# Edge loop of a graph layer: three banks for the edge products, one softmax step per item, key rows from DRAM, sums two places later

## The reference, cut to what matters

```python
q, k, v = x @ Wq + bq, x @ Wk + bk, x @ Wv + bv       # per node
e = edge_attr @ We                                      # per edge
kj = k[src] + e
alpha = einsum('ehc,ehc->eh', q[dst], kj) / sqrt(C)
amax = segment_max(alpha, dst)
ea = exp(alpha - amax[dst])
denom = segment_sum(ea, dst)
msg = (v[src] + e) * (ea / (denom[dst] + 1e-16))[:, :, None]
out = segment_sum(msg, dst) + (x @ Ws + bs)
```

## Time and profile before

| | us |
|---|---|
| Median of three runs | 2544.61 |
| Profiled execution, its own time | 2543.3 |
| Its span | 2541.5 |
| TensorE busy | 2375.7 |
| VectorE busy | 2029.1 |
| GpSimd busy | 1809.0 |
| ScalarE busy | 1573.9 |
| Edge loop, first to last projection | 224.8 to 1925 |

### The profile page before, as it was taken

How to read it: one execution, slowest core, us unless ns; L and a number is a source line. 1 busy time by engine, 2 the same in 40 slices (tenths; PEclk the granted TensorE clock), 3 DMA queues, 4 the chain that set the end, 5 groups by cost and what they waited for, 6 DMA issues and landing times. The chain is left out here.

```text
span 2541.5 us, 61885 instructions
## 1 busy us (share of the span) xinstructions
PE 2375.7 (93%) x13314; PEld 1998.8 (79%) x13315; DVE 2029.1 (80%) x5248; ACT 1573.9 (62%) x4349; POOL 1809.0 (71%) x2136
## 2 busy tenths in 40 slices
PE   6998999999999999999999999999996658999998
PEld 3445888888888888888888888888884647999998
DVE  6865999999999999999999999999997873222222
ACT  1223677776777677777777777776775115666665
POOL 4213788888888888888888888888886204666666
PEclk9999999999999999999999999999998558999999
DMA  7326777777777777777778777777772672433443
GB/s 233 129 106 197 234 229 224 228 228 224 223 228 228 219 229 228 223 228 226 228 226 230 228 223 228 226 228 215 230 225 82 203 215 57 71 63 64 69 67 54
DMA packets 337727, 476.35 MB, mean 187 GB/s; under 512 B 61382, under 2 KB 268556, under 8 KB 337116
## 3 DMA queue, kind: packets, MB, share of 16 engines
q0 software_dynamic: 92576, 259.72, 38.4%
q1 hardware_dynamic: 238556, 213.23, 27.7%
q10 hardware_dynamic: 6288, 0.05, 0.1%
HBM read 425.40 MB, written 50.57 MB: 187 GB/s over the span
## 5 line engine op out<-in xcount | busy, mean ns | idle before, releaser
L809 POOL DMA_INDIRECT kv_ring<-vk_table,tab_c x880 | 860.0, 977 | 274.9 <-issue 176.5
L967 PE MATMUL ps_e<-we_sb,aT 128*128 128x256 f32 x3520 | 917.8, 384 | 23.8 <-DVE ve_ke L1055 19.9
L967 PEld LDWEIGHTS ps_e<-we_sb,aT 128*128 128x128 f32 x3520 | 602.0, 191 | 95.6 <-issue 46.3
L1050 DVE TENSOR_TENSOR ve_ke<-kv_ring,ps_e 128x512 f32<-128x512 f32 x880 | 599.7, 681 | 34.1 <-PE ps_e L971 22.7
L819 POOL TENSOR_TENSOR ve_ke<-ve_ke 128x256 f32<-128x256 f32 x880 | 551.2, 630 | 16.5 <-ACT factor L936 3.0
L1020 PE MATMUL ps_u<-ve_ke,sel 128*128 128x264 f32 x1760 | 545.3, 392 | 17.0 <-POOL ve_ke L819 6.1
L971 PE MATMUL ps_e<-q_slots,selT 128*128 x1760 | 517.5, 375 | 0.0
L896 ACT COPY aT<-ps_t 128x256 f32<-128x256 f32 x880 | 325.4, 370 | 294.6 <-PE ps_t L951 255.3
L1126 DVE SCALAR_TENSOR_TENSOR node_slots<-node_slots,same_tile,ps_u 128x264 f32 x880 | 422.6, 480 | 25.5 <-PE ps_u L1020 21.4
L971 PEld LDWEIGHTS ps_e<-q_slots,selT 128*128 128x128 f32 x1760 | 335.3, 191 | 45.1
L1038 DVE TENSOR_REDUCE alpha<-ve_ke 128x8 f32<-128x256 f32 x880 | 362.4, 412 | 1.9
(11 more groups left out here) (251 smaller groups left out, 2630.3 us busy)
## 6 DMA issues: line engine op xcount, KB each, us to landing
a_ring<-in_edge_attr SPq DMA_DIRECT2D x880, 128.0 KB
loc_c<-loc_table SPq DMA_DIRECT2D x220, 128.0 KB, 4.4
kv_ring<-vk_table,tab_c POOLq DMA_INDIRECT x880
vk_table<-kv_out SPq DMA_DIRECT2D x49, 256.0 KB, 2.0
skip_table<-skip_out SPq DMA_DIRECT2D x49, 128.0 KB, 1.7
skip<-skip_table SPq DMA_DIRECT2D x7, 896.0 KB, 9.3
xn_table<-node_slots SPq DMA_DIRECT2D x7, 896.0 KB, 5.1
w_sb<-in_L_ffn_W SPq DMA_DIRECT2D x2, 2048.0 KB, 10.3
```

The lines of the kernel that those rows point to most:

```text
L809: g.indirect_dma_start(out=kv_ring[:, i % N_KV, :], out_offset=None, in_=vk_table, in_offset=bass.IndirectOffsetOnAxis(ap=tab_c[:, c % N_T ...
L967: t.matmul(ps_e[i % 2][:, 0:D], aT[i % 2][:, k * P:(k + 1) * P], we_sb[:, k, :], start=(k == 0), stop=(k == KD - 1))
L1050: v.tensor_tensor(ve_ke[:, to:ke + 1:ke - to, 0:D], kv.rearrange("p (t d) -> p t d", t=2), e[:, None, :].to_broadcast([P, 2, D]), ALU.add) ...
```

## The change

- `N_E = 3`: the edge products go to three banks in turn, `ps_e[(c * CH + i) % 3]`, and a projection waits for VectorE's reads of the item three back.
- All softmax products share one bank `ps_s`: the scores, then the minima; the turned result takes the place of the scores.
- The key rows are no longer turned by TensorE. The first section writes two tables of 8 values per item to DRAM (`first_table`, `last_table`), and SyncE loads them, spread over the partitions, once per chunk into `key_c`. The previous chunk's last key is part of that row, so `key_prev` goes.
- `minima` has two transposes and one product of 8 columns where it had three transposes.
- Places: TensorE from keys 0, scores 3, minima 6, turn_scores 10 to scores 4, minima 7, turn_scores 12. ScalarE's `exp` from 11 to 12. VectorE from scan 3, scan_back 4, own 6, least 7, shift 8 to scan 3, scan_back 4, own_first 6, own_last 7, least_first 8, least_last 9, shift 10.
- Lags: select from 11 to 13, sum and add from 13 to 15; weigh stays at 15.
- The addition is `source + ps_u`, where a second slot number per item names the source: the item's own node slot, or, at the first item of a node tile, a slot of zeros. The numbers are loaded as pairs, for two items at a time, within the score of an item.
- Later sections place some buffers over others; their instructions stay.

```diff
             LAG = dict(weigh=FIRST_WEIGH + N_KV,
-                       select=FIRST_WEIGH,
-                       sum=FIRST_WEIGH + 2,
-                       add=FIRST_WEIGH + 2)
+                       select=FIRST_WEIGH + 2,
+                       sum=FIRST_WEIGH + 4,
+                       add=FIRST_WEIGH + 4)
...
-                over_chunks(act, emit, what="select", parts={3: "apart", 4: "offs", 11: "exp"})
+                over_chunks(act, emit, what="select", parts={3: "apart", 4: "offs", 12: "exp"})
...
-                    pe.wait_ge(s["kq_ready"], at("kq_ready", c * CH + (i - 2)))
+                    pe.wait_ge(s["kq_ready"], at("kq_ready", c * CH + (i - N_E)))
...
-                            t.transpose(ps_r[:, KW - P:KW], min_l[par][:, 0:1].to_broadcast([P, P]), ident[:, :])
                             t.transpose(ps_r[:, 0:P], scan_b[:, 0:1].to_broadcast([P, P]), ident[:, :])
-                            t.transpose(ps_r[:, P:2 * P], scan_f[:, P - 1:P].to_broadcast([P, P]), ident[:, :])
+                            t.matmul(ps_r[:, P:P + H], min_l[par][:, 0:1].to_broadcast([P, P]), ident[:, P - H:P], start=True, stop=True)
+                            t.transpose(ps_r[:, P + H:KW], scan_f[:, P - 1:P].to_broadcast([P, P]), ident[:, :])
...
-                over_chunks(pe, emit, what="sum", parts={0: "keys", 3: "scores", 6: "minima", 10: "turn_scores"})
+                over_chunks(pe, emit, what="sum", parts={4: "scores", 7: "minima", 12: "turn_scores"})
...
+            def load_keys(sp, c):
+                keys = key_c[c % 2]
+                sp.dma_start(keys[:, 0:P], first_table[c * CH:(c + 1) * CH, :].rearrange("(o i) h -> o (i h)", o=1).to_broadcast([P, P])
+                             ).then_inc(key_loaded[c % 2], 16)
+                sp.dma_start(keys[:, P:KW], last_table[c * CH:(c + 1) * CH + 1, :].rearrange("(o i) h -> o (i h)", o=1).to_broadcast([P, P + H])
+                             ).then_inc(key_loaded[c % 2], 16)
...
+                then(v.scalar_tensor_tensor(out=from_rep[:, :], in0=node_tile_rep[:, :], scalar=float(NT + 2), in1=same_tile[:, :],
+                                            op0=ALU.subtract, op1=ALU.mult))
+                for h in range(2):
+                    row, some = slice(64 + 32 * h, 65 + 32 * h), slice(h * IT // 2, (h + 1) * IT // 2)
+                    v.tensor_copy(item_slots[h][:, :, 0], node_tile_rep[row, some])
+                    then(v.tensor_scalar(item_slots[h][:, :, 1], from_rep[row, some], float(NT + 2), None, ALU.add))
...
+                def slots_of(c, i):
+                    h, m = divmod(c * CH + i, IT // 2)
+                    both = nc.values_load_multi_w_load_instructions(
+                        item_slots[h][:, m:m + AT_ONCE, :].rearrange("p i k -> p (i k)"), engines=[mybir.EngineType.DVE],
+                        min_val=0, max_val=NT + 2, skip_runtime_bounds_check_because="a count of at most NT steps, or NT + 2")[1]
+                    return list(zip(both[0::2], both[1::2]))
...
-                    v.scalar_tensor_tensor(out=to, in0=sofar, scalar=same_tile[:, m:m + 1], in1=ps_u[i % 2][:, 0:UW], op0=ALU.mult, op1=ALU.add
-                                           ).then_inc(s["acc_added"], 1)
+                    v.tensor_tensor(to, sofar, ps_u[i % 2][:, 0:UW], ALU.add).then_inc(s["acc_added"], 1)
...
-                over_chunks(dve, emit, what="add", parts={3: "scan", 4: "scan_back", 6: "own", 7: "least", 8: "shift"})
+                over_chunks(dve, emit, what="add", parts={3: "scan", 4: "scan_back", 6: "own_first", 7: "own_last",
+                                                         8: "least_first", 9: "least_last", 10: "shift"})
```

More of the change, by code:

```diff
@@ L22 @@
 N_KV = 4
+N_E = 3
 N_A = 4
@@ L99, in gnn_ffn @@
         item_row = item_rows[32:33, :]
+        item_slots = [item_rows[64 + 32 * h:65 + 32 * h, :].rearrange("p (i k) -> p i k", k=2) for h in range(2)]
         chunk_tile = sb("chunk_tile", [P, NCH])
@@ L131, in gnn_ffn @@
         run_c = [sb(f"run_c{i}", [P, P], F32, c_soft) for i in range(2)]
+        KW = 2 * P + H
+        key_c = [sb(f"key_c{i}", [P, KW], F32, c_soft) for i in range(2)]
         resets = [sb(f"resets{i}", [P, P + 1], F32, c_soft) for i in range(2)]
@@ L136, in gnn_ffn @@
         reset_loaded = [sem(f"reset_loaded{i}", c_soft) for i in range(2)]
+        key_loaded = [sem(f"key_loaded{i}", c_soft) for i in range(2)]
         loc_loaded = [sem(f"loc_loaded{i}", c_soft) for i in range(NLOC)]
@@ L176, in gnn_ffn @@
             t_rep = sb1("t_rep", [P, IT])
+            from_rep = t_rep
             t_item = sb1("t_item", [P, IB])
@@ L313, in _ @@
                     if j == LOCS_OUT:
+                        with nc.allow_non_contiguous_dma(reason="eight head keys of an item"):
+                            keys_to_tables()
                         sp.wait_ge(tables_ready, LOCS)
@@ L1121, in add @@
-                def add(c, i, n, before):
+                AT_ONCE = 2
+                assert CH % AT_ONCE == 0 and IT // 2 % AT_ONCE == 0
+                def slots_of(c, i):
[4 more added lines that the diff above has]
+                    return list(zip(both[0::2], both[1::2]))
@@ L1129, in emit, with load_next @@
                 def emit(c, par, steps):
+                    adds = [(c - b, k) for kind, k, b in steps if kind == "add"]
+                    places = len([1 for kind, k, b in steps if kind == "score"])
+                    def load_next(place):
+                        if adds and place + len(adds) >= places:
+                            cc, k = adds.pop(0)
+                            if k % AT_ONCE == 0:
+                                ahead[:] = slots_of(cc, k)
                     for kind, i, back in steps:
@@ L1590, in gnn_ffn @@
             y_full = [sb7(f"y_full{i}", [P, D]) for i in range(2)]
-            y = [sb7(f"y{i}", [P, D]) for i in range(4)]
+            y = [values[:, i, :] for i in range(4)]
             ps_t = [c7.enter_context(nc.psum_tensor(f"ps_t7{i}", [P, 512], F32)) for i in range(2)]
```

140 lines of the change are left out of this document (73 added, 67 removed).

## The result

| | median us | range | runs |
|---|---|---|---|
| before | 2545.75 | 2544.28 to 2549.65 | 4 |
| after | 2585.91 | 2583.47 to 2587.03 | 4 |

The changed kernel is slower: ratio 1.0154, 95% interval 1.0136 to 1.0172. I had said 2529 (2500 to 2556), with 0.15 for slower. The profiled span is 2581.6 us, 40.1 longer than before.

What follows compares the result with a forecast made beforehand. TensorE and VectorE were taken as nearly full, with waits deciding. Per chunk 1.72 us go and 1.35 come, net -0.37, times 54 is -20.0; prologue and tail +3.6, together -16: 2529 us, range 2500 to 2556.

Steps and rivals of the forecast that it cites:

- The copy behind the exponentials: TensorE's projection 13 waits for ScalarE's copy 13, queued behind the exponentials: 1.25 us taken per chunk.
- X + 1.90: Forecast start of projection 13; X is the start of TensorE's sum after turn_scores, copy end X + 1.84 plus 0.06 us.
- Register loads: VectorE's eight loads of 4 slot numbers per chunk hide behind the wide addition: 0 us taken, bounds 0 to 2.8.
- The sums at lag 15 ... no sum for the weighing: TensorE's sum gets four places of slack behind GpSimd's weighing instead of two; the 0.38 us wait at place 3 goes.
- the second rival: VectorE stays as late; sums wait for the addition two items back, 0.3 us a chunk, time 2545; chance 0.14.
- The plain addition: VectorE's add takes 0.41 us instead of 0.480, saving 1.1 us a chunk.
- the 0.2 that I had taken off: On VectorE, one softmax step per item removes the wait of 0.2 us between the two own steps, an estimate.
- what was gone: TensorE's savings per chunk: key transposes 0.32 us and waits at places 3, 9 and the chunk boundary 1.2 us.
- Prologue: Five added operations ahead of the first statistics, on the path to the first projection: 2.6 us.
- GpSimd "is not next": GpSimd needs some 28.8 us a chunk with the mask, below what TensorE keeps, so it does not become the bound.
- The register-load rival: Each slot load holds up VectorE behind it; at 0.43 us each the time is 2602; chance 0.10.
- the clock rival: The 1.2 us wait lowers TensorE's clock in each chunk, costing 0.7 us more, time 2567; chance 0.03.

Runs made afterwards that it cites:

- the mixed order: Changed kernel with minima 6, turn_scores 10, exponentials 11, own and least undivided at 6 and 7, shift 8; scores 4 and sums' lag 15 kept: 2541.39 us.
- old order: Changed kernel with every place and lag as before the change, all the changed data kept: 2527.33 us, ratio 0.9927.
- the second experiment: Changed kernel with TensorE's register load of 16 slot numbers issued behind the projection of place 8 instead of 13: 2562.91 us, ratio 1.0071.
- the mixed order with lag 13: The mixed order with select back at lag 11 and sums and additions at 13 instead of 15: 2563.30 us, ratio 1.0062.

## Why the prediction was wrong

**The copy behind the exponentials: right.** 1.25 us forecast; measured 1.18 by the idle marks and 1.20 by place; X + 1.89 in the median where X + 1.90 was forecast. It needed only the order of the steps and four durations of ScalarE.

**The term that failed is the rest of that step: "Register loads".** I followed VectorE's loads, which cost nothing as said (0.34 us for four numbers), and left out TensorE's own, whose row stood beside them. I had costed it implicitly at nothing. It was hidden only where it stood behind queued work, and my own new wait stands right before it. It costs 0.41 us at place 13, 22 us over the chunks; moved to place 8 it gives back 23 us. That the two agree is in part luck, since a part of the wait at place 1 went with it and waits for edge tiles came.

**"The sums at lag 15 ... no sum for the weighing": the second rival, under-priced.** It named the mechanism, two banks for the sums, gave it 0.3 us and a chance of 0.14. Measured: 0.35 + 0.13 + 0.09 = 0.57 us at places 1, 10 and 11, about 31 us. With lag 15 the rescale falls into VectorE's step 15, beside the chunk's last reduction. I had budgeted VectorE by its sum per chunk (28.6 against 30.6), but a wait is decided at a place: from that step's wide addition to the next one it takes 3.37 us in the kernel after and 3.15 in the mixed order, where it takes 2.04 with the reduction alone (old order) and TensorE's pace is 1.77. The sum was off as well: VectorE is busy 31.61 x 1495.3/1600 = 29.5 us a chunk. The plain addition saved 1.0 of the 1.1 said, but the 0.6 us that other instructions lose beside GpSimd's work came on top, and the 0.2 that I had taken off was a wait, not work.

These two make the chunk 1.0 us longer than the 30.6 forecast: 54 of the 57 us between 2529 and 2586. They are not independent: the second experiment shows that the 0.35 at place 1 goes when the load moves. The sign follows: what was gone (0.32 keys, 1.2 waits) was as forecast, what came was 1.20 + 0.06 and another 1.0.

**Prologue: 2.6 forecast, 5.4 measured.** With the five added operations VectorE begins its first statistics 2.3 us later, near what was worked out. The other 3 appear late in the projection stage, where TensorE waits 4.08 us once for the normalised rows where it waited 2.95. Right behind that wait the granted clock is 0.50, which is 1.2 GHz, for 3.4 us (before the change it was 1.00 in this stretch). The stretch, columns as above:

```profile
213.80:217.20 3.40, 3.40 (x5) 1.35 (x4) 0.95 (x3) 0.66 (x2) 0.72 (x1) 0.50 0.40 144
```

Its weight loads stand 0.86 us apart and not 0.43. So my estimate of the 3 is 1.1 for the longer wait and some 1.7 for the clock. What made the wait longer was not tried.

**GpSimd "is not next": wrong, and unseen in this result.** I had compared 28.8 us with TensorE's chunk, again a sum. TensorE waits for GpSimd at place 3 (excess 1.15 us) in the old order and in the mixed order with lag 13, and halving its weighing in the mixed order wins 29 us. Whether another order would go below 2527 us was not tried.

**The other rivals.** The register-load rival did not occur: VectorE's loads stay hidden. Nor did the clock rival in the middle of the loop: the clock is 1.00 from 300 to 1900 us with a wait of 1.16 us in every chunk. It did occur once, in the first chunks: after a wait of 2.17 us for the same copy the clock is 0.50 from 282.1 to 285.4 us, and a projection's four weight loads take 1.33 us.

**Open.** The third bank was worth 47 us in the new order and 10 in the mixed one; I have not separated why. The irregular waits were not explained, except those for edge tiles. How much of the time goes back to VectorE's instructions beside GpSimd's was not tested.

## What to carry to other kernels

When a change puts a wait into an in-order engine, list what follows the waiting instruction on that engine's own sequencer (register loads above all): a part of what was hidden behind queued work is added to the wait (0.41 of 1.10 us here). Budget a nearly full engine by place, not by the sum over the loop: a lump that moves next to another lump is late there, however much the sum has fallen. When three engines take 1.77 to 1.85 us per item, a change of order mostly moves a wait from one to the next. The orders tried with the changed data and three banks for the edge products lie between 2527 and 2586 us; work taken off two engines (half a product and half a weighing) gave 2478. And look at the duration of instructions that the change only moves: here three of them grew by 0.2 to 0.4 us each in the mean.

## What the runs showed of the hardware

A register load takes 0.34 us for 4 numbers and 0.60 for 8 (on VectorE's sequencer) and 1.10 for 16 (on TensorE's): 0.063 us a number above 0.09, one line for all three. The load of 16 cost nothing at place 8, and 0.41 of its 1.10 us right behind a projection that had been waited for. An F32 addition of SBUF and PSUM over 264 columns takes 0.419 us plain and 0.480 as a fused multiply and add. GpSimd's weighing fell from 0.627 to 0.410 us when its columns were halved, VectorE's product from 0.409 to 0.277. An indirect gather holds GpSimd for 0.98 us in the mean, in the kernel before, the kernel after and the runs with halves left out. A VectorE instruction with both operands in SBUF that starts while GpSimd weighs lasts until 0.16 us (`least`, 0.62 us for 0.35) or 0.29 us (the rescale's wide product in the kernel before, 0.65 for 0.42) after the weighing's end. TensorE's granted clock fell to 0.50 right after single waits of 2.17 and 4.08 us, but not after one of 2.95 us in the kernel before, nor with waits of 1.16 us in each chunk.
